# adaLN block with attention and a routed LoRA FFN: another order of the first loads and tiles, and v of batches 2 and 3 made first and turned by VectorE and DMA

## What is computed

```python
mod = (silu(c) @ wmod).reshape(4, 6, 1, 512)            # sa, ca, ga, sb, cb, gb
ga = (2 * (ga >= 0) - 1) * maximum(abs(ga), 0.25)       # gb in the same way
h = layernorm(x) * (1 + ca) + sa
q, k, v = split(h @ Wqkv + bqkv)                        # 128 wide each
x = x + ga * (softmax(q @ k.T / sqrt(128)) @ v @ Wo + bo)
h = layernorm(x) * (1 + cb) + sb
e = argmax(h @ gate_w.T + expert_bias)                  # one of 4 experts
x = x + gb * (h @ W_up.T + lora_B[e] @ (lora_A[e] @ h))
```

## Time and profile before

| | us |
|---|---|
| median of 3 runs (lowest, highest) | 183.2 (183.02, 183.76) |
| profiled execution, whole | 182.96 |
| its span | 181.2 |
| TensorE busy | 170.8 (94%) |
| VectorE busy | 139.6 (77%) |
| ScalarE busy | 90.1 (50%) |
| GpSimd busy | 80.4 (44%) |

### The profile page before, as it was taken

The page is one execution under the profiler, slowest core; times in us unless marked ns, Lnnn a source line. Parts: engine busy times, 40 slices in busy tenths (PEclk is TensorE's granted clock), DMA queues, the critical chain, the costliest instruction groups (busy, mean ns, idle before and its releaser), DMA issues.

```text
span 181.2 us, 2841 instructions
## 1 busy us (share of the span) xinstructions
PE 170.8 (94%) x924; PEld 134.9 (74%) x924; DVE 139.6 (77%) x352; ACT 90.1 (50%) x170; POOL 80.4 (44%) x109
## 2 busy tenths in 40 slices
PE   6867999999999999999999999999999999999990
PEld 5845655978758778878687777788887878768890
DVE  3647759998888988978999929699388285988965
ACT  3347124975167895139349562713487512483100
POOL 3374200179452719240988960017695000362650
PEclk9999999999999999999999999999999999999999
DMA  3999998851014002344020763001140000001415
GB/s 130 313 352 379 387 385 234 269 206 52 0 54 183 0 0 50 98 109 157 0 114 33 213 139 83 0 0 56 65 149 26 0 2 0 0 4 58 174 41 190
DMA packets 13918, 21.32 MB, mean 118 GB/s; under 512 B 3356, under 2 KB 4128, under 8 KB 13904
## 3 DMA queue, kind: packets, MB, share of 16 engines
q1 hardware_dynamic: 13904, 21.15, 35.1%
HBM read 14.83 MB, written 4.21 MB: 105 GB/s over the span
## 4 chain that ended last, share of the span: by engine, by line
PE 57%; DVE 18%; ACT 8%; SPq 6%; DMA 6%; issue 4%; POOL 0%; DVEq 0%; ACTq 0%; POOLq 0%
PE bank L400 37%; SPq L322 5%; DMA stage<-in_L_wmod_dram 4%; PE bank L414 3%; DVE xs L1236 3%; ACT xn_p L849 3%; DVE stats L1243 3%; DVE xn L1169 2%; PE bank L524 2%; DVE f_gb L1301 1%; DVE h1lo L1158 1%; DVE h2lo L1174 1%; PE bank L509 1%; PE bank L503 1%; DMA stage<-xn 1%
## 5 line engine op out<-in xcount | busy, mean ns | idle before, releaser
L400 PE MATMUL bank<-wup_lo,h2hi 128*128 128x512 f32 (+1 forms) x68 | 27.2, 401 | 0.4 <-ACT h2hi L907 0.4
L400 PE MATMUL bank<-wup_hi,h2hi 128*128 128x512 f32 (+1 forms) x68 | 26.0, 382 | 0.0
L888 ACT ACTIVATE xn_p<-xs,shift,rstd 128x512 f32<-128x512 f32 x16 | 13.1, 816 | 25.9 <-POOL shift L1498 25.8
L400 PE MATMUL bank<-wup_hi,h2lo 128*128 128x512 f32 (+1 forms) x68 | 25.9, 381 | 0.0
L1495 POOL TENSOR_TENSOR rstd<-var_eps,neg_half 128x1 f32<-128x1 f32 x16 | 8.9, 554 | 37.2 <-DVE var_eps L1247 37.2
L1510 POOL TENSOR_TENSOR xs<-xs,f_gb 128x512 f32<-128x512 f32 x14 | 17.9, 1292 | 7.7 <-DVE f_gb L1301 7.7
L400 PE MATMUL bank<-h1lo,wqkv_hi 128*128 128x512 f32 x48 | 19.7, 411 | 1.6 <-ACT wqkv_hi L881 1.2
L1487 POOL TENSOR_TENSOR xs<-xs,gabo 128x512 f32<-128x512 f32 x16 | 20.3, 1308 | 0.1
L400 PE MATMUL bank<-h1hi,wqkv_hi 128*128 128x512 f32 x48 | 19.0, 395 | 0.0
L400 PE MATMUL bank<-h1hi,wqkv_lo 128*128 128x512 f32 x48 | 18.9, 394 | 0.0
L1219 DVE TENSOR_TENSOR plo<-bank,phi 128x512 fp32r<-128x512 f32 x16 | 10.0, 684 | 6.7 <-ACT phi L857 6.6
(11 more groups left out here) (185 smaller groups left out, 410.0 us busy)
## 6 DMA issues: line engine op xcount, KB each, us to landing
out_dram<-xs SPq DMA_DIRECT2D x15, 256.0 KB, 2.0
stage<-in_L_wmod_dram SPq DMA_DIRECT2D x3, 1024.0 KB, 8.0
xs<-in_L_wmod_dram SPq DMA_DIRECT2D x3, 1024.0 KB, 7.6
xs<-in_L_attn_x_dram SPq DMA_DIRECT2D x3, 1024.0 KB, 8.4
stage<-xn SPq DMA_DIRECT2D x32, 64.0 KB, 2.0
f_gb<-in_L_ffn_W_up_dram SPq DMA_DIRECT2D x1, 1024.0 KB, 11.4
gb_bc<-gates_dram SPq DMA_DIRECT2D x4, 256.0 KB, 4.1
xn_p<-in_L_attn_Wqkv_dram SPq DMA_DIRECT2D x4, 192.0 KB, 6.5
```

Of the source, the lines that this page charges most:

```text
L400: mm = nc.tensor.matmul(dst, w, m, start=first and i == 0, stop=last and i == total - 1)
L888: nc.scalar.activation(xn2_p[:, t, :], xs[:, b, t, :], ACT.Identity, bias=shift[:, 1, t:t + 1], scale=rstd[:, 1, t:t + 1]).then_inc(S["xn2 ...
```

## The change

Five things are changed.

- Loads: x of batch 0 comes in two halves, and SyncE's two waits among the first loads are gone.
- First tiles: tile 1 is turned ahead of `modulation(0)`, tile 3 behind the first half of the ca columns; one filler product is gone.
- ga: `first_gate_everywhere` uses transposes in place of products.
- Gate product: `gate_ffn(b-1, 0)` stands ahead of `ln2_moments(b, 0)` in batches 1 and 2, behind it before.
- v of batches 2 and 3: TensorE makes v ahead of q and k; ScalarE evicts it between the second and third tile of `ln2_normalise`, with its tokens in order (`v_to_blocks`); VectorE turns it within 32x32 blocks in place (`turn_v`), between tiles 2 and 3 of the residuals; SyncE moves the blocks into fb_hi with 16 DMAs of 32 partitions x 512 B (`move_v`), ahead of the output rows; ScalarE and VectorE then make v_hi and v_lo from SBUF. The TensorE transposes of v and their bank are left out for these batches.

```diff
@@ psum_plan
-        order += [(m[t], "S", b, t) for t in range(NT)] + [(m[4], "V", b)]
+        order += [(m[t], "S", b, t) for t in range(NT)] + ([(m[4], "V", b)] if b < TURNED else [])
@@ names
+        v_rows = fb_hi[:].rearrange("p (a t i) -> p t a i", a=NB, t=NT)
+        def v_there(engine, b):
+
+            engine.wait_ge(v_moved, 16 * NB * NB * (b - TURNED + 1))
@@ SyncE
+            def move_v(b):
+
+                sp.wait_ge(S["v_turned"], b - TURNED + 1)
+                sp.wait_ge(S["fb_rows_ready"], 1)
+                if b > TURNED:
+                    sp.wait_ge(S["v_lo_ready"], b)
+                for a in range(NB):
+                    for c in range(NB):
+                        sp.dma_start(fb_hi[c * BLOCK:(c + 1) * BLOCK, a * P:(a + 1) * P],
+                                     vT[a * BLOCK:(a + 1) * BLOCK, c * P:(c + 1) * P]).then_inc(v_moved, 16)
+
-            for i, ts in enumerate((slice(0, 1), slice(1, 2), slice(2, 4))):
-                sp.dma_start(xs[:, 0, ts], x_v[0, :, ts, :]).then_inc(x0_in[i], 16)
+            for i in range(2):
+                sp.dma_start(xs[:, 0, 2 * i:2 * i + 2], x_v[0, :, 2 * i:2 * i + 2, :]).then_inc(x0_in[i], 16)
             load_section("ca")
-            sp.wait_ge(x0_in[1], 16)
             load_wqkv((0, 1))
-            sp.wait_ge(x0_in[2], 16)
             load_section("sa")
@@ SyncE, loop over b
                 if b == 1:
                     move_turned(3)
+                if b + 2 < B:
+                    move_v(b + 2)
@@ TensorE
-                    mm = nc.tensor.matmul(dst[:, kt * P:(kt + 1) * P], gate_col[:, 0, kt, 0:1].to_broadcast([P, P]), ident[:],
-                                          start=True, stop=True)
+                    mm = nc.tensor.transpose(dst[:, kt * P:(kt + 1) * P], gate_col[:, 0, kt, 0:1].to_broadcast([P, P]), ident[:])
@@ TensorE, loop over b
                 scores(b)
-                v_transposes(b)
                 if b == 1:
+                    v_transposes(1)
                     gate_shift_columns()
...
-                    qkv(b + 1, range(NK))
+                    qkv(b + 1, range(NK), (2,))
+                    qkv(b + 1, range(NK), (0, 1))
@@ ScalarE
+            def v_to_blocks(b):
+
+                act.wait_ge(S["qkv_psum"], 3 * b + 1)
+                if b == TURNED:
+                    act.wait_ge(S["V_psum"], b)
+                else:
+                    v_there(act, b - 1)
+                nc.scalar.activation(vT[:].rearrange("p (c t i) -> p t c i", c=NB, t=NT),
+                                     at("qkv", b, 2)[:].rearrange("p (t c i) -> p t c i", c=NB, t=NT), ACT.Identity,
                                      bias=qb[:, 2, b:b + 1]).then_inc(S["vT_ready"], 1)
...
+                if b >= TURNED:
+                    v_there(act, b)
+                    nc.scalar.activation(v_hi[:].rearrange("p t (a i) -> p t a i", a=NB), v_rows, ACT.Copy).then_inc(S["v_hi_ready"], 1)
+                    return
@@ VectorE
+            def turn_v(b):
+                dve.wait_ge(S["vT_ready"], b + 1)
+                nc.vector.transpose(vT[:], vT[:]).then_inc(S["v_turned"], 1)
```

More of the change, by code:

```diff
@@ L198, in adaln_block @@
         wqkv_in = [sem(f"wqkv_in{kt}") for kt in range(NK)]
-        x0_in = [sem(f"x0_in{i}") for i in range(3)]
+        x0_in = [sem(f"x0_in{i}") for i in range(2)]
         x_in = [sem(f"x_in{b}") for b in range(B)]
@@ L204, in adaln_block @@
         turned_moved = sem("turned_moved")
+        v_moved = sem("v_moved")
         stored = sem("stored")
@@ L216, in adaln_block @@
             ln1_stats ln1_aggr ln1_var ln1_rstd ln1_shift xn1_ready xn1_by_act xn1_turned x1T_psum h1_hi h1_lo
-            qkv_psum qk_hi_ready qk_lo_ready vT_ready V_psum v_hi_ready v_lo_ready S_psum max_ready
+            qkv_psum qk_hi_ready qk_lo_ready vT_ready v_turned V_psum v_hi_ready v_lo_ready S_psum max_ready
             negmax_ready p_ready PT_psum pt_hi pt_lo O_psum o_hi_ready o_lo_ready inv_ready Y_psum
@@ L696, in _ @@
             keep_warm(bank[4], 2)
+            first_x1_transposes((1,))
             modulation(0)
-            first_x1_transposes((1,))
-            keep_warm(bank[5], 1)
             first_x1_transposes((2,))
+            first_modulation_columns(0)
             first_x1_transposes((3,))
-            first_modulation_columns(0)
             first_modulation_columns(1)
@@ L817, in qkv_evacuate @@
                 for j in range(2):
-                    act.wait_ge(S["qkv_psum"], 3 * b + j + 1)
+                    act.wait_ge(S["qkv_psum"], 3 * b + j + (1 if b < TURNED else 2))
                     if b:
@@ L997, in _ @@
                 if not last:
-                    ln2_normalise(b)
+                    ln2_normalise(b, (0, 1))
+                    v_to_blocks(b + 1)
+                    ln2_normalise(b, (2, 3))
                     wo_high(b + 1)
@@ L1019, in ln1_stats @@
                     if b == 0:
-                        dve.wait_ge(x0_in[min(t, 2)], 16)
+                        dve.wait_ge(x0_in[t // 2], 16)
                     else:
@@ L1199, in qk_low @@
                     low.then_inc(S["qk_lo_ready"], 1)
+            def turn_v(b):
+                dve.wait_ge(S["vT_ready"], b + 1)
+                nc.vector.transpose(vT[:], vT[:]).then_inc(S["v_turned"], 1)
             def v_low(b):
                 dve.wait_ge(S["v_hi_ready"], b + 1)
+                if b >= TURNED:
+                    high = v_hi[:].bitcast(F32).rearrange("p t (a i) -> p t a i", a=NB)
+                    nc.vector.tensor_tensor(v_lo[:].rearrange("p t (a i) -> p t a i", a=NB), v_rows, high,
+                                            ALU.subtract).then_inc(S["v_lo_ready"], 1)
+                    return
                 nc.vector.tensor_tensor(v_lo[:].rearrange("p t d -> p (t d)"), at("V", b)[:],
@@ L1399, in _ @@
                         residual(b, t)
+                        if t == 0:
+                            gate_ffn(b - 1, 0)
                         ln2_moments(b, t)
-                        if t != 1:
-                            gate_ffn(b - 1, (0, 0, 1, 2)[t])
+                        if t >= 2:
+                            gate_ffn(b - 1, t - 1)
+                        if t == 2:
+                            turn_v(b + 1)
                     gate_ffn(b - 1, 3)
```

10 lines of the change are left out of this document (6 added, 4 removed).

## The result

| | us |
|---|---|
| kernel before, median of 8 runs (lowest, highest) | 182.89 (182.42, 184.97) |
| changed kernel, median of 8 runs (lowest, highest) | 184.82 (183.80, 185.10) |
| ratio, 95% interval | 1.0102 (1.0079 to 1.0126) |
| changed kernel, profiled execution, whole and span | 183.8, 182.1 |

The change makes the kernel 1.0% slower. The forecast was 184.3, and 184.36 for the profiled execution, which took 183.8 and was the quickest of the eight; the median lies 0.5 above the forecast. So the total is close, but two of its terms are not, and they err in opposite directions: the start gained more than was forecast, and v of batch 3 cost more.

A forecast was written before the change was run, and what follows sets the result against it. TensorE was taken as the bound, busy 170.8 of 181.2 us, with VectorE arriving at the same moment around batch 1. 182.96 minus 0.5, plus 1.05, plus 0.85 is 184.36, stated as 184.3; range 182.1 to 186.1.

The forecast's parts named there:

- The start: Start of the program: earlier loads and the new tile order save 0.5 us, with bounds 0 and 1.0.
- signs of being wrong: Turns of vT without a wait, x of batch 1 landing before 18, or ScalarE waiting for v's pieces.
- Its last sentence: If the first load stream moved as a whole, the start alone would give more than both batches take.
- ga: The ga spread before pv of batch 0: 0.6 us saved becomes a longer wait; counted 0, bound 0.26.
- Batch 1: Making v of batch 2 first: VectorE's wait of 0.3 and turn of 0.7 cost 1.05 us.
- Batch 2: Making v of batch 3 first: VectorE waits some 2.2 us for v; adds 0.85 us, bounds 0.4 and 1.5.
- this sign of the prediction: VectorE idles about 2 us just before the turn of v of batch 3.
- the small DMAs: Sixteen 16 KB pieces per batch on SyncE take 12.1 us from the turn; counted 0, all margins thin.
- The other margins: Pieces of v land before v_hi wants them: by 0.7 us for batch 2, 0.2 for batch 3.
- The rival of the late pieces: DMAs take 0.1 us more each or land late, delaying v_hi(3) 1.6; 1.9 more, 186.2 us; chance 0.13.

The follow-up runs named there:

- the two runs that removed the wait: The change with v moved by one transfer per batch, 183.36 us; the change with gate spreads and xn pieces ahead of batch 0's outputs on SyncE, 183.63 us.
- the later turn: The change with VectorE's turn of v behind residual 3, its moments and the gate product: 188.62 us, ratio 1.031 to the kernel before.
- both edits: The change with v turned behind residual 3, and gate spreads and xn pieces ahead of batch 0's outputs on SyncE: 185.26 us, ratio 1.014.
- without v: The whole change except its v part, with TensorE transposing v of all batches as before: 181.52 us, ratio 0.993 to the kernel before.
- the order alone: The change with v made first and evicted early but transposed by TensorE, without VectorE's turn or SyncE's pieces: 181.61 us, ratio 0.994.

## Why the prediction came out as it did

**The start: direction right, size wrong.** 0.5 was forecast, with 1.0 as the upper bound; 1.64 by the two first traces, 1.4 over all traces. By the medians it is 1.2 together with the gate product. The step that failed is "what can be won is only what is left of gaps in the stream, a tenth of the 7 us". A busy share of nine tenths in slices of 4.5 us hid a stretch at 0.76 and 180 GB/s; 2 us at half rate, and a tenth more rate behind it, are about the 1.47 us by which x of batch 1 lands sooner in the first pair of traces (1.05 on average over all). The prediction also left ca where it was, with modulation(0) at 10.59; it started at 9.87, and so qkv of batch 0 at 13.97 and not at 14.6. The rest of the step is right: the landing of x of batch 1 is what sets the gain. Two of its signs of being wrong came, x landing before 18 and no idle time at the qb columns. Its last sentence named the stream moving as a whole as the case in which the whole would be wrong. It came, without its consequence: both batches cost 2.5 and not less than the start gives.

**ga: 0.** The wait ahead of pv of batch 0 rose from 0.26 to 0.7, as it had said, and the gain at pv (1.65) is that of qkv (1.64). No run had this edit alone.

**Batch 1: right.** 1.05 forecast for v, 1.04 measured; the parts too, a wait of 0.3 (0.39) and a turn of 0.7 (0.71), with the order costing nothing of its own. The gate product took 0.16 back, where the prediction had put it at nothing because the bank that it frees "is no longer the last thing": batch 1 as a whole costs 0.88 against the kernel before, and 1.05 where v is the only edit. That qkv(2) would start at the second residual held as well (waits 0.85).

**Batch 2: mechanism half right, size too small.** 0.85 forecast, 1.49 measured. The wait of 2.2 us for v exists, 2.28 and 2.30 where the queue on SyncE is mended, and this is what is then left: 41.33 - 40.64, **0.69**, near the 0.85. In the changed kernel it is 0.37, so this sign of the prediction failed. The step that failed is the one on the small DMAs: "ScalarE's h1_hi of batch 3 ... waits 1.7 ... I count 0". It waited 2.46, and the two runs that removed the wait show its price, 0.80. The prediction worked out that the bank would be free at 124.9 and TensorE come at 125.0, a margin of 0.1 us, and counted nothing. But the pieces of xn start 4.9 us later than before, both counted from pv of batch 1 (33.70 for 28.81), where 4.1 had been worked out; h1_high waits 0.76 us longer than forecast, and the bank comes 0.40 after TensorE. With qkv(3) v, its turn and residual 3 are late. How the 1.49 divide depends on what is taken away first: the queue and then the turn give 0.80 and 0.69, the turn and then the queue 0.36 and 1.13.

**The other margins** were estimated well. V of batch 2 was in time. Of batch 3, the last issue is at 138.7 with 1.8 to landing, 140.5, and v_hi starts at 140.55: in time by 0.1 (by 0.4 in the second trace, 141.1 and 141.51). The runs with the later turn show the far side. Counted from pv of batch 1, the turn is 1.9 us later in batch 2 and 3.7 in batch 3, the second partly because of the first, and the stretch of batch 2 grows by 3.6. With both edits it is 1.9 and 1.4 later, and the stretch grows by 1.6. The rival of the late pieces had the mechanism; it only was not what this change does. Its price, 1.9 us, is near what batch 2 loses with both edits, 1.6, and half of what it loses with the later turn alone, and it lacked the 1.6 us more that the clock takes.

**The 0.88 us saved on TensorE** bought nothing in any trace: without v, with its eight transposes in place, the kernel is, with the order alone (0.9937), the fastest of all that ran, 181.52, 0.7% under the kernel before and 1.3% under the change (by the ratios 0.9934 and 1.0066). It is the version to keep. The rule of the Trainium skill that the prediction weighed (VectorE: DVE Perf Modes, Rules for kernel authors: TensorE for a 128x128 transpose when PSUM will do) is borne out by more than the prediction gave it: the four transposes that TensorE had done in 0.44 us cost 1.04 and 1.49 on the other path.

| step | forecast | measured |
|---|---|---|
| start | -0.5 | -1.64 (first traces), -1.4 (all) |
| ga | 0 | 0 |
| batch 1 | +1.05 | +0.88: v 1.04, gate product -0.16 |
| batch 2 | +0.85 | +1.49, SyncE's queue and VectorE's wait and turn, which overlap |
| sum, profiled execution | 184.36 | 183.8 |

Before's first trace plus these, 182.96 - 1.64 + 0.88 + 1.49, is 183.7, against 183.8; the last 0.1 is in the stretch to the end. That the total came out within 0.6 us is luck in part: the start was 1.1 us off in this pair of traces, batch 2 0.64 the other way, and the gate product 0.16 was not in the sum.

## What to carry to other kernels

Look at a load stream in stretches of a microsecond or two and in GB/s, not by its busy share in forty slices: a wait in the issuing queue showed here as 180 and 242 GB/s at three quarters of the share, where 362 and 370 were moved without it. When a transposition is moved from a full TensorE to another engine, ask who waits behind the turn in that engine's queue and what stands behind the pieces in the issuing queue; here 0.44 us a batch was saved for 1.0 and 1.5. A margin that is worked out as a few tenths is a cost with a chance and belongs in the sum: behind sixteen DMAs one such margin, of 0.1, was 0.8 us, and another, overrun by a turn made 1.9 and 3.7 us later, was over four.

## What the runs showed of the chip that was not expected

- SyncE's SBUF to SBUF pieces cost it 0.59 us each whatever they carry: the 16 KB pieces of v and the 64 KB pieces of xn have the same median, and start 0.63 apart in the chain. Making them smaller saved SyncE nothing here; one transfer of 256 KB took 0.5 us of issue.
- Two executions of one kernel differ by up to 1.15 us in the start alone, by how the first loads land, and keep that distance to within 0.1 us through batch 1 (0.2 by the end of batch 2). A difference between two kernels is better read stretch by stretch than from the ends of two traces.
- After 2.2 us in which TensorE had nothing to do, late in the kernel, the granted clock went from 1.00 to 0.50 and was back at 0.92 between 150 and 152; the wait cost 1.6 us more than its own length. A second kernel with 2.17 us of idle in the same place shows the same, and 2.24 us of idle near the start of a kernel left the clock at 1.00.
